# Row statistics of a perceiver's layer norms: from one batch per slot to eight batches at the head of each stage

## What is computed

```python
def _layernorm(x, axis=-1, eps=1e-05):
    m = jnp.mean(x, axis=axis, keepdims=True)
    v = jnp.var(x, axis=axis, keepdims=True)
    return (x - m) / jnp.sqrt(v + eps)

x = x + L0_xattn(_layernorm(x), ctx)   # 8 heads, swishmax over 2048 keys, values down and up
x = x + L0_attn(_layernorm(x))         # 16 heads, difference of two softmaxes, layer norm of the output
x = x + L0_ffn(_layernorm(x))          # own layer norm, attention, residual, layer norm, 8 experts (top 2)
x = x + L1_xattn(_layernorm(x), ctx)   # 16 heads, softmax over 2048 keys
x = x + L1_attn(_layernorm(x))         # 16 heads, positive random features
x = x + L1_ffn(_layernorm(x))          # 64 scalar nets
```

## Time and profile before

| | before |
|---|---|
| median of 3 runs | 4335.48 us (4335.45 to 4336.42) |
| the profiled execution | 4337.49 us |
| its span, first to last instruction | 4335.7 us |
| TensorE busy (matmul) | 4154.6 us, 96% |
| VectorE busy | 2078.4 us, 48%, 4510 instructions |
| ScalarE busy | 1400.0 us, 32% |
| GpSimd busy | 237.8 us, 5% |
| mean granted TensorE clock | 0.980 |
| instructions | 62686 |

### The profile page before, as it was taken

The page is one execution under the profiler, slowest core; times in us unless marked ns, Lnnn a source line. Parts: engine busy times, 40 slices in busy tenths (PEclk is TensorE's granted clock), DMA queues, the critical chain, the costliest instruction groups (busy, mean ns, idle before and its releaser), DMA issues. The chain is left out here.

```text
span 4335.7 us, 62686 instructions
## 1 busy us (share of the span) xinstructions
PE 4154.6 (96%) x25216; PEld 2806.2 (65%) x25216; DVE 2078.4 (48%) x4510; ACT 1400.0 (32%) x3796; POOL 237.8 (5%) x247
## 2 busy tenths in 40 slices
PE   9999999999999999999888999999999999998887
PEld 5767676767676767676465444666666666666775
DVE  4333333333333333255454333666666666656556
ACT  3222222222222222134223101444444444433333
POOL 0000000000000000022210000000000000000212
PEclk9999999999999999999999999999999999999899
DMA  5010101110101010210300500101101101101000
GB/s 175 30 49 30 49 30 49 30 49 30 49 30 49 30 49 30 84 40 20 122 20 20 180 0 24 50 16 52 52 18 50 52 23 45 50 1 42 11 1 20
DMA packets 86438, 189.74 MB, mean 44 GB/s; under 512 B 7696, under 2 KB 17552, under 8 KB 84368
## 3 DMA queue, kind: packets, MB, share of 16 engines
q1 hardware_dynamic: 72976, 137.55, 9.4%
q0 software_dynamic: 13184, 48.24, 3.6%
HBM read 168.99 MB, written 16.78 MB: 43 GB/s over the span
## 5 line engine op out<-in xcount | busy, mean ns | idle before, releaser
L510 PE MATMUL swishmax_attended<-swishmax_weights_t,swishmax_context 128*128 128x256 f32 x4096 | 905.1, 379 | 0.0
L510 PEld LDWEIGHTS swishmax_attended<-swishmax_weights_t,swishmax_context 128*128 128x128 f32 x4096 | 769.7, 190 | 98.0
L525 PE MATMUL swishmax_bank<-ahead_stream,swishmax_w_key 128*128 128x512 f32 x1024 | 475.9, 608 | 7.1 <-DMA ahead_stream<-in_context_t_dram 7.1
L1435 PE MATMUL context_bank<-ahead_stream,ahead_staged 128*128 128x512 f32 x1024 | 473.1, 605 | 1.3 <-PEq L1010 1.3
L1303 ACT ACTIVATE context_exps<-context_score,context_neg_max 128x512 f32<-128x512 f32 x512 | 344.7, 685 | 397.3 <-DVE context_neg_max L1332 397.3
L391 ACT ACTIVATE swishmax_xes<-swishmax_score,swishmax_neg_max 128x512 f32<-128x512 f32 x256 | 164.4, 687 | 846.7 <-DVE swishmax_neg_max L423 846.7
L423 DVE TENSOR_REDUCE swishmax_neg_max<-swishmax_score 128x1 f32<-128x512 f32 x256 | 164.8, 685 | 434.4 <-PE swishmax_score L496 434.2
L525 PEld LDWEIGHTS swishmax_bank<-ahead_stream,swishmax_w_key 128*128 128x128 f32 x1024 | 185.5, 191 | 287.1 <-issue 284.1
L1332 DVE TENSOR_REDUCE context_neg_max<-context_score 128x1 f32<-128x512 f32 x512 | 317.5, 682 | 108.2 <-PE context_score L1403 108.0
L1435 PEld LDWEIGHTS context_bank<-ahead_stream,ahead_staged 128*128 128x128 f32 x1024 | 184.4, 190 | 280.5 <-issue 273.7
L1450 PEld LDWEIGHTS context_bank<-whole_ident,context_exps 128*128 128x128 f32 x2048 | 230.7, 142 | 131.8 <-issue 70.0
(11 more groups left out here) (319 smaller groups left out, 4947.2 us busy)
## 6 DMA issues: line engine op xcount, KB each, us to landing
ahead_stream<-in_context_t_dram SPq DMA_DIRECT2D x78, 1024.0 KB, 5.4
swishmax_context<-in_context_dram POOLq DMA_DIRECT2D x32, 1024.0 KB, 5.8
ahead_values<-ahead_staged SPq DMA_DIRECT2D x14, 1024.0 KB, 8.4
context_values<-ahead_values POOLq DMA_DIRECT2D x56, 256.0 KB, 3.6
experts_w<-in_L_ffn_W_dram SPq DMA_DIRECT2D x16, 512.0 KB, 8.9
whole_x<-in_x_dram SPq DMA_DIRECT2D x8, 256.0 KB, 10.6
swishmax_down<-_L_xattn_value_down_dram SPq DMA_DIRECT2D x8, 256.0 KB, 4.9
swishmax_up<-in_L_xattn_value_up_dram SPq DMA_DIRECT2D x1, 2048.0 KB, 10.2
```

Source lines behind the costliest of these rows:

```text
L510: last = nc.tensor.matmul(attended[m // 2][:, m % 2, :], context[:, c, k, m * P:(m + 1) * P], weights_t[:, n % 2, k].rearrange("p r q -> p ...
L525: last = nc.tensor.matmul(bank_t[:], w_key[:, k, g * P:(g + 1) * P], context_t[:, c, k, :], start=k == 0, stop=k == DC - 1)
L1435: last = nc.tensor.matmul(bank_t[:], w["k"][:, k, g * P:(g + 1) * P], context_t[:, c, k, :], start=k == 0, stop=k == DC - 1)
```

## The change

`row_stats` and `tile_stats` go. `RowStats` gets `gather`, which for a list of batches does a bn_stats each and then a bn_aggr each, with one link behind each group, and `finish`, which does the inverse square root for a whole range of batches in 13 instructions with one column per batch; `take` is both. The places where it is called move: all eight batches at the head of twin, plain (with the eight first normalisations and the statistics of `mid`), experts and context; batch 0 at the head of swishmax and the other seven at its second unit. The features and nets stages cannot have their input that early: their batches 0 to 6 are gathered one at a time once each output tile is done, in the stage before, and finished together at the end or in halves; the last batch of features is taken in features' slot 2, the last of nets at the head of nets.

```diff
@@ row_stats and tile_stats are removed @@
 class RowStats:
     def __init__(self, s, name):
-        self.stats, self.work = s.sb(name + "_stats", [P, 6]), s.sb(name + "_work", [P, 2])
-        self.mv, self.rstd = s.sb(name + "_mv", [P, B, 2]), s.sb(name + "_rstd", [P, B])
-
-    def take(self, nc, link, b, x):
-        row_stats(nc, link, x, self.stats[:], self.mv[:, b, :], self.work[:], self.rstd[:, b:b + 1])
+        self.stats, self.mv = s.sb(name + "_stats", [P, B, 6]), s.sb(name + "_mv", [P, B, 2])
+        self.var, self.half = s.sb(name + "_var", [P, B]), s.sb(name + "_half", [P, B])
+        self.tmp, self.rstd = s.sb(name + "_tmp", [P, B]), s.sb(name + "_rstd", [P, B])
+
+    def gather(self, nc, link, batches, x):
+        for b in batches:
+            last = nc.vector.bn_stats(self.stats[:, b, :], x[:, b, :])
+        link(last)
+        for b in batches:
+            last = nc.vector.bn_aggr(self.mv[:, b, :], self.stats[:, b, :])
+        link(last)
+
+    def finish(self, nc, link, batches):
+        cols = slice(batches[0], batches[-1] + 1)
+        var, half, tmp, y = self.var[:, cols], self.half[:, cols], self.tmp[:, cols], self.rstd[:, cols]
+        link(nc.vector.tensor_scalar(var, self.mv[:, cols, 1], LN_EPS, None, ALU.add))
+        nc.vector.tensor_scalar(half, var, -0.5, None, ALU.mult)
+        link(nc.vector.tensor_scalar(tmp.bitcast(U32), var.bitcast(U32), 1, None, ALU.logical_shift_right))
+        link(nc.vector.tensor_scalar(y.bitcast(I32), tmp.bitcast(I32), -1.0, float(RSQRT_SEED), ALU.mult, ALU.add))
+        for _ in range(RSQRT_STEPS):
+            link(nc.vector.tensor_tensor(tmp, y, y, ALU.mult))
+            link(nc.vector.tensor_tensor(tmp, tmp, half, ALU.mult))
+            link(nc.vector.scalar_tensor_tensor(out=y, in0=tmp, scalar=1.5, in1=y, op0=ALU.add, op1=ALU.mult))
+
+    def take(self, nc, link, batches, x):
+        self.gather(nc, link, batches, x)
+        self.finish(nc, link, batches)
@@ swishmax_context @@
-            out += [("stats", b + 1)] * (g == 1 and c == 0 and b + 1 < B) + [("norm", b + 1)] * (g == 1 and c == 2 and b + 1 < B)
+            out += [("stats", 1)] * (n == NCH) + [("norm", b + 1)] * (g == 1 and c == 2 and b + 1 < B)
...
-                        rows_of_x.take(nc, link, u, x_sb[:, u, :])
+                        rows_of_x.take(nc, link, range(u, B if u else 1), x_sb)
@@ token_attention (twin and plain) @@
-            out += [("scale", t - 1, 1, 1)] * (c and SETS == 2) + [("output", t - 2, 0)] * o
-            return out + [("stats", t + 2)] * (t + 2 < B)
+            return out + [("scale", t - 1, 1, 1)] * (c and SETS == 2) + [("output", t - 2, 0)] * o
...
-        dve_steps = [("stats", 0), ("norm", 0), ("stats", 1)] + [x for t in range(B + 2) for x in dve_slot(t)]
+        dve_steps = [("norm", 0)] + [x for t in range(B + 2) for x in dve_slot(t)]
...
-                def set_lambda():
-                    dve.wait_ge(loaded, 16 * LOADS)
+                rows_of_x.take(nc, first, range(B), x_sb)
+                if not twin:
+                    for b in range(B):
+                        last = rows_of_x.apply(nc, source[:, b, :], b, x_sb)
+                    first(last)
+                    rows_of_mid.take(nc, first, range(B), source)
+                dve.wait_ge(loaded, 16 * LOADS)
+                if twin:
                     for n in range(2):
                         first(nc.vector.tensor_tensor(lam_in[:, 2 * n, :], ...
...
-                    if what == "stats":
-                        rows_of_x.take(nc, link, b, x_sb[:, b, :])
-                        if not twin:
-                            link(rows_of_x.apply(nc, source[:, b, :], b, x_sb[:, b, :]))
-                            rows_of_mid.take(nc, link, b, source[:, b, :])
-                        elif b == 1:
-                            set_lambda()
-                        continue
@@ experts @@
-                tile_stats(nc, first, mid, stats, mv, tmp[:], rstd[:], var[:])
-                first(nc.vector.tensor_copy(means[:], mv[:, :, 0]))
+                rows_of_mid.take(nc, first, range(B), mid)
+                first(nc.vector.tensor_copy(means[:], rows_of_mid.mv[:, :, 0]))
@@ softmax_context @@
-            out += [("stats", b + 1)] * (g == 0 and c == 2 and b + 1 < B) + [("norm", b + 1)] * (g == 1 and c == 0 and b + 1 < B)
-            out += [("later_stats", 0)] * (n == NU * NCH)
+            out += [("norm", b + 1)] * (g == 1 and c == 0 and b + 1 < B)
+            out += [("later", b - 1)] * (g == 1 and c == 2 and b >= 1)
...
+                rows_of_x.take(nc, first, range(B), x_sb)
+                dve.wait_ge(loaded, 16 * LOADS)
+                first(nc.vector.tensor_scalar(bias_q[:], bias[:, 0, :], SCALE, None, ALU.mult))
...
+                    elif what == "later":
+                        dve.wait_ge(out_d, ring.count(("output", u)))
+                        later.rows.gather(nc, link, [u], x_sb)
+                        if u == B - 2:
+                            later.rows.finish(nc, link, range(B - 1))
@@ kernel_attention (features) @@
-            return out + [("stats", t + 2)] * (t + 2 < B) + [("later_stats", t - 2)] * o
+            return out + [("stats", B - 1)] * (t == 2) + [("later", t - 2)] * (o and t < B + 1)
...
-        dve_steps = [("norm", 0), ("stats", 1)] + [x for t in range(B + 2) for x in dve_slot(t)]
+        dve_steps = [("norm", 0)] + [x for t in range(B + 2) for x in dve_slot(t)]
...
-                        later.rows.take(nc, link, b, x_sb[:, b, :])
+                        later.rows.gather(nc, link, [b], x_sb)
+                        if b == B // 2:
+                            later.rows.finish(nc, link, range(B // 2))
@@ scalar_nets @@
-                for b in range(B):
-                    own.rows.apply(nc, hidden[:, b, :], b, x_sb[:, b, :]).then_inc(normed_x, 1)
+                for b in range(NB):
+                    own.rows.apply(nc, hidden[:, b, :], b, x_sb).then_inc(normed_x, 1)
+                link = Chain(dve, chain)
+                own.rows.gather(nc, link, [B - 1], x_sb)
+                own.rows.finish(nc, link, range(NB, B))
+                for b in range(NB, B):
+                    own.rows.apply(nc, hidden[:, b, :], b, x_sb).then_inc(normed_x, 1)
```

More of the change, by code:

```diff
@@ L145, in layer_norm @@
     return nc.vector.tensor_scalar(out, x, mv[:, 0:1], y, ALU.subtract, ALU.mult)
-def row_stats(nc, link, x, stats, mv, work, y):
-    var, tmp, minus_half = mv[:, 1:2], work[:, 0:1], work[:, 1:2]
-    link(nc.vector.bn_stats(stats, x))
-    link(nc.vector.bn_aggr(mv, stats))
-    link(nc.vector.tensor_scalar(var, var, LN_EPS, None, ALU.add))
-    link(nc.vector.tensor_scalar(minus_half, var, -0.5, None, ALU.mult))
-    link(nc.vector.tensor_scalar(tmp.bitcast(U32), var.bitcast(U32), 1, None, ALU.logical_shift_right))
-    link(nc.vector.tensor_scalar(y.bitcast(I32), tmp.bitcast(I32), -1.0, float(RSQRT_SEED), ALU.mult, ALU.add))
-    for _ in range(RSQRT_STEPS):
-        link(nc.vector.tensor_scalar(tmp, y, y, minus_half, ALU.mult, ALU.mult))
-        link(nc.vector.tensor_scalar(y, tmp, 1.5, y, ALU.add, ALU.mult))
@@ L205, in merged @@
     return out
-def tile_stats(nc, link, x, stats, mv, tmp, rstd, var):
-    for b in range(B):
-        last = nc.vector.bn_stats(stats[:, b, :], x[:, b, :])
-    link(last)
-    for b in range(B):
-        last = nc.vector.bn_aggr(mv[:, b, :], stats[:, b, :])
-    link(last)
-    link(nc.vector.tensor_copy(var, mv[:, :, 1]))
-    rsqrt(nc, link, var, tmp, rstd, LN_EPS)
-STATS_LINKS = 3 + 3 + 4 * RSQRT_STEPS
 def tile_at(tile, turn, n=1):
@@ L1069, in _ @@
                         b = i * NB + n
-                        link(nc.vector.tensor_scalar(tokens[:, n, :], columns(mid, b), tile_at(means, b), tile_at(rstd, b),
+                        link(nc.vector.tensor_scalar(tokens[:, n, :], columns(mid, b), tile_at(means, b), tile_at(rows_of_mid.rstd, b),
                                                      ALU.subtract, ALU.mult))
@@ L1354, in _ @@
                         nc.vector.tensor_scalar(heads_t[:, b % 2, g, :], attended[:], bias[:, 2, g:g + 1], None, ALU.add).then_inc(heads_out, 1)
-                    elif what == "stats":
-                        rows_of_x.take(nc, link, u, x_sb[:, u, :])
-                        if u == 0:
-                            dve.wait_ge(loaded, 16 * LOADS)
-                            first(nc.vector.tensor_scalar(bias_q[:], bias[:, 0, :], SCALE, None, ALU.mult))
-                    elif what == "later_stats":
-                        later.rows.take(nc, link, u, x_sb[:, u, :])
+                    elif what == "later":
[3 more added lines that the diff above has]
+                            later.rows.finish(nc, link, range(B - 1))
                     elif what == "norm":
-                        rows_of_x.apply(nc, hidden[:], u, x_sb[:, u, :]).then_inc(normed_x, 1)
+                        rows_of_x.apply(nc, hidden[:], u, x_sb).then_inc(normed_x, 1)
```

22 lines of the change are left out of this document (11 added, 11 removed).

## The result

The changed kernel takes 4236.13 us (median of 4 runs, 4235.70 to 4237.23), the kernel before, run beside it, 4335.95 (4 runs, 4335.45 to 4337.20): ratio 0.977, 95% interval 0.9753 to 0.9787. The forecast was 4241.9, within 4230 to 4269. The profiled execution of after took 4237.23 us, its span is 4235.4, against 4335.7 before: 100.3 us less. The medians differ by 99.8, where the prediction had 93.6.

A forecast was written before the change was run, and what follows sets the result against it. TensorE, busy 4154.6 of 4335.7 us, was taken as the bound, so only its idle or half-clocked time could be won. Terms 19.0 - 0.5 + 34.5 + 31.2 + 10.4 - 1 = 93.6 off 4335.48 gave 4241.9 us, range 4230 to 4269.

The forecast's parts named there:

- taking slot 7 as the model of slots 3 to 6 of twin and 2 to 6 of plain: Twin and plain: slots behind a call shrink to the call-free slot's length, saving 19.0 us in twin and 31.5 in plain.
- rival A: Whole kernel: only waits come back, not the clock; 66.5 us saved, so 4269; chance 0.09.
- so a call costs 3.38 us ... TensorE stands 2.44 us: Twin slot 5: VectorE's statistics call delays the maxima 3.38 us, and TensorE waits 2.44 us for ScalarE's queued copy.
- Twin head: Start of twin: two calls and a normalisation (7.3 us) become an 8.7 us burst; 0.5 us lost.
- the rule: Twin head: skill-page timing gives eight bn_stats 5.5 us, not 4.85; loss 1.2, sum 4242.7; the prediction used the row.
- Rival C: Stage heads: bursts not covered, dear tensor_scalars make each 12.4 us; 23 us lost, 4358 with no gain; chance 0.04.
- Plain head: Start of plain: bursts, normalisations and GpSimd take 26.2 us, TensorE wants the result after 27.6; covered, 1.4 to spare.
- Features: Features stage: 31.2 us saved, summed over slots 4 to 6, 3, 1, 2, 8 and 9, and the last call.
- Context: Context stage: 10.4 us saved, 7 from key-eviction waits and the rest from the call at the last unit.
- Swishmax, experts, nets: These three stages: swishmax 0, experts 0, nets 1 us lost.
- B: Whole kernel: nothing is won because another wait in the same slot takes its place; 4335 us; chance 0.02.
- D: Context and features: a gather delays a slot like a call, losing 7 and 19 us; 4268 us; chance 0.05.

The follow-up runs named there:

- e7: Changed kernel plus a dummy chain of 15 VectorE instructions, about 3.35 us, at the end of twin slots 0 to 5: 4251.62 us.
- e3: Changed kernel plus a dummy chain of six VectorE instructions, about 1.7 us, at the end of twin slots 0 to 5: 4244.78 us.
- e6: Changed kernel plus one unused bn_stats of 0.69 us at the end of twin slots 0 to 5: 4237.81 us.
- e11: The changed kernel again, unedited, as a control: 4235.18 us.
- e8: Changed kernel plus one old call of 3.38 us in the last steps of the context stage: 4240.16 us.
- e1: Changed kernel with the old batch-by-batch calls back in twin and plain, placed ahead of the second half's maxima instead of at the slot's end: 4244.99 us.
- e2: Changed kernel with plain's eight batches still at the stage's head, but each with the old chained calls instead of batched: 4271.15 us.

## Why the prediction was right, and where its terms were off

The mechanism and the number were both right: calls ahead of the maxima cost delay and clock, and moving them gave both back. The total was nearer than its terms. Of the 6.7 us by which the profile beat the forecast, context alone gave 5.6 and nets 2.4, while twin and features fell short by 1.6 and 1.0.

**The slots.** Right to a tenth: taking slot 7 as the model of slots 3 to 6 of twin and 2 to 6 of plain gave 140.92 for 140.86 and 118.40 for 118.41. It worked since it compared slots and not waits; had it added up waits, it would have been rival A, which the clock of 1.00 in plain refutes. That the half-clock time went with the waits was argued in the prediction; e7 shows it for twin, and for plain and features it rests on their own slot 7. The step "so a call costs 3.38 us ... TensorE stands 2.44 us" left the impression of slack; e3 and e6 show none.

**Twin head.** Forecast 0.5 lost, measured 2.0 (49.23 before, 51.21 after, from first spare tile to first score). The wait grew only from 2.02 to 2.38; the other 1.6 us is the low clock behind it, which the term didn't have. By the Trainium skill's VectorE page (VectorE: DVE Perf Modes, section The DRAIN you can't avoid) the eight bn_stats would have taken 5.5 us; that section measured copies, and it also says that an operation which isn't held back starts earlier. The row at the twin head says 4.85 again, so the rule doesn't fit these eight and the loss has another cause. (With the rule the prediction's sum comes to 4242.6, not 4242.7.) VectorE's timeline, after:

```profile
1755.68 4.85 DVE L158 BATCH_NORM_STATS2 twin_x_stats<-whole_x 128x6 f32<-128x512 f32 x8 [0.42 <-PEq L328]
1760.56 0.64 DVE L161 BATCH_NORM_AGGREGATE twin_x_mv<-twin_x_stats 128x2 f32<-128x6 f32 x8
...
1763.73 0.42 DVE L786 TENSOR_TENSOR twin_lam_in<-twin_lam_in 128x32 f32<-128x32 f32 x2
```

The burst takes 8.05 us (8.7 forecast at most). Rival C's dear tensor_scalar of 1.18 us doesn't appear at the heads of twin, plain and context: they take 0.17 there. It does appear where GpSimd is adding at that time. In the experts head of after (GpSimd busy from 2341.14 to 2351.00) the four take 0.54, 1.19, 1.32 and 1.19 us, in nets one takes 1.19:

```profile
2347.38 1.19 DVE L168 TENSOR_SCALAR experts_mid_half<-experts_mid_var 128x8 f32<-128x8 f32 x1
```

Experts' spare tiles cover it: the stage is as long as before. So rival C's price is real, and the rows agree with the prediction's reason against it, that GpSimd is idle in the other heads. No run moved GpSimd's work, so the cause of the price isn't tested.

**Plain head.** "Covered with 1.4 us to spare": right, no wait before the first transposes at 2134.84. GpSimd was done at 2130.43, so 4.4 us were spare: two bursts and eight normalisations took 19.9 us for the 22.9 at most that I had (operations on eight columns follow each other after 0.20 us, not 0.245). Slot 1 gave 3.3 for the 3 that I took.

**Features.** 30.2 for 31.2, by terms that err both ways: slots 4 to 6 18.6 for 19.0 (the residue is 0.64 us a slot, not 0.5); slot 3 2.7 for 4, as the forecast wait of 2.5 came (2.47 measured) but 1.4 us of low clock stood behind it; slot 1 4.7 for 2.3, of which the wait gave the 2.3 (4.44 to 2.15) and the clock the rest; slot 2 0.3 lost for 0.5 won; the head 0.6 won, which had no term; the last call 3.6 for 3.4; slots 8 and 9 0.3 for 2. e11 puts a bound to such reading: 5.5 us of the stage are chance.

**Context.** The largest miss: 16.0 for 10.4. The body gave 9.3 for 7: the first six batches became 1.2 to 1.9 us shorter each (mostly 161.7 to 160.2 from output tile to output tile), and the seventh, where gather and finish stand in place of the call, stayed at 178.0. The waits for keys fell by 6.8 us (7.9 to 1.1), as forecast, and those for the scaled weights' copies, which had no term, from 1.5 to 0.4; no named wait shows the other 1.4. The stage's end gave 6.7 for 3.4, because the term was the wait's length alone; e8 measures the call there at 5.7, as much as these rows differ between before and after (5.6); the last 1.1 lies ahead of it and is not explained. I had counted clock time in the slots, where it could be read from slot 7, and forgotten it where a single wait was priced by its row. The same omission is in the twin head and in slots 1 and 3 of features.

**Swishmax, experts, nets.** 0.7, 0.2 and 1.4 saved. Swishmax's burst of seven batches cost TensorE nothing. Nets was forecast 1 longer and came out 1.4 shorter, but e11 has it at 38.5, 1.0 longer, and the nine edited kernels have it at 37.6 to 37.9; its term can't be settled at this size.

The rivals: A and B are refuted by the slots; C by the heads that leave TensorE no new wait in plain and one of 2.38 for 2.02 in twin; D (a gather delays like a call) by features slots 4 to 6. A gather isn't free there either: 0.64 us of its 0.9 remain in each slot, and e6 shows in twin that 0.7 us in front of the maxima are paid in full.

## What to carry to other kernels

In-order work of an engine that is half idle costs by its place: 46 us of it cost 4.3 us in the two stages where it stood apart (e1), and each us of it ahead of the awaited step cost at least a us (e3, e6, e7). So first look what stands directly ahead of the step that the other engines wait for, and move that. A slot of the same kernel that lacks the suspect is a better measure of its cost than the waits in the profile, as it holds the delay and the clock together. Work moved to a stage's head must be short enough for the cover there (e2), so the move to the head and the batching belong together. Calls left as they were, at an idle place of the slot, gave most of the gain too (e1).

## What the runs showed that was not expected

A wait costs more than its length where the clock falls behind it. Sixteen matmuls of 1.96 us took 3.65 after a wait of 3.43; in twin slots with waits of 0.8 us the clock stayed at 1.00 (e3, e6), in those with 2.4 it was 0.96 (e7). It is not a fixed price. In the last units of context in after, waits of 2.60 and 2.72 us (matmuls at 3917.45 and 3924.36) had matmuls at full speed behind them. And behind features' wait of 2.5 us the 32 matmuls took 1.94 us in after's profile and 1.08 in e11's:

```profile
4025.65 1.94 PE L1745 MATMUL features_bank<-features_features_t,features_sums 128*32 128x128 f32 x32 [2.47 <-ACT features_features_t L1607]
```

So one profile of one kernel carries an error of some 5 us in a stage with many waits (features 251.3, 251.4 and 245.8 for the same instructions), while stages at full clock repeat to 0.1 us (plain 234.1, 234.1, 234.0). What decides where a low stretch falls was not found.
